# Dequantized FFN weights in a macaron block: gate and up weights by bytes, 1024 wide in PSUM, low halves on VectorE, gathers in sections of 1, 4 and 6 tiles

## The reference

```python
def _dequant(qw, qz, sc, g_idx):
    shifts = jnp.arange(8, dtype=jnp.uint32) * 4
    wq = qw[:, None, :] >> shifts[None, :, None] & NIB
    wq = wq.reshape(-1, qw.shape[1]).astype(jnp.float32)
    zq = qz[:, :, None] >> shifts[None, None, :] & NIB
    zq = zq.reshape(qz.shape[0], -1).astype(jnp.float32) + 1.0
    return sc[g_idx] * (wq - zq[g_idx])
w_gu = _dequant(qweight_gu, qzeros_gu, scales_gu, g_idx_gu)      # 512 x 2752
inter = jnp.einsum('bsh,hf->bsf', x, w_gu)
gate, up = (inter[..., :INTER], inter[..., INTER:])              # INTER = 1376
h = jax.nn.silu(gate) * up
w_d = _dequant(qweight_down, qzeros_down, scales_down, g_idx_down)
return jnp.einsum('bsf,fh->bsh', h, w_d)

x = x + 0.5 * ffn(layernorm(x))
x = x + attention(layernorm(x))
x = x + 0.5 * ffn(layernorm(x))
```

## Time and profile before

| what | value |
|---|---|
| median of 3 runs (lowest, highest) | 660.63 us (659.92, 666.45) |
| profiled execution, its own time | 665.29 us |
| its span, first to last instruction | 663.5 us |
| TensorE busy, share of the span | 583.2 us, 88% |
| VectorE, ScalarE, GpSimd busy | 384.8, 281.8, 86.1 us |
| mean granted TensorE clock | 0.969 |

### The profile page before, as it was taken

The page is one execution under the profiler, slowest core; times in us unless marked ns, Lnnn a source line. Parts: engine busy times, 40 slices in busy tenths (PEclk is TensorE's granted clock), DMA queues, the critical chain, the costliest instruction groups (busy, mean ns, idle before and its releaser), DMA issues.

```text
span 663.5 us, 8621 instructions
## 1 busy us (share of the span) xinstructions
PE 583.2 (88%) x3024; PEld 439.4 (66%) x3024; DVE 384.8 (58%) x886; ACT 281.8 (42%) x816; POOL 86.1 (13%) x87
## 2 busy tenths in 40 slices
PE   1087988889999997797898898888999999999998
PEld 1065866658888885574574575545588887888886
DVE  7377999982331138889879979999121133411113
ACT  2132223231112135888998999799211111211111
POOL 4777545430000000000000000000000000000000
PEclk9997999998999999696999998989999999999999
DMA  6967334229600001103002001100590000100001
GB/s 165 285 194 215 109 99 127 76 76 277 296 1 1 0 1 32 33 1 64 2 1 56 9 1 33 34 0 2 160 331 1 1 0 1 64 0 1 0 1 64
DMA packets 44627, 46.71 MB, mean 70 GB/s; under 512 B 12636, under 2 KB 37318, under 8 KB 43816
## 3 DMA queue, kind: packets, MB, share of 16 engines
q1 hardware_dynamic: 39888, 35.51, 18.3%
q0 software_dynamic: 2656, 10.57, 5.3%
q10 hardware_dynamic: 2040, 0.08, 0.2%
HBM read 31.72 MB, written 10.30 MB: 63 GB/s over the span
## 4 chain that ended last, share of the span: by engine, by line
PE 61%; DVE 20%; ACT 6%; issue 6%; POOL 5%; ACTq 1%; DMA 0%; DVEq 0%; POOLq 0%
PE bank L1023 29%; PE bank L1038 14%; PE bank L1139 4%; DVE sc L861 4%; PE bank L1105 3%; DVE wf L700 3%; PE bank L1069 3%; ACT sc L560 3%; POOL zs L397 2%; DVE raw L690 2%; DVE wf L704 2%; DVE qp L832 2%; DVE nmax L870 2%; PE bank L1123 1%; ACT pt L575 1%
## 5 line engine op out<-in xcount | busy, mean ns | idle before, releaser
L712 DVE TENSOR_TENSOR hf<-sil,bank 128x512 f32<-128x512 f32 (+1 forms) x44 | 30.1, 685 | 178.9 <-PE bank L1023 178.9
L1038 PE MATMUL bank<-w_d,hs 128*128 128x512 f32 (+1 forms) x528 | 130.1, 396 | 2.1 <-ACT hs L496 1.3
L560 ACT ACTIVATE sc<-sc,nmax 128x128 f32<-128x128 f32 (+1 forms) x256 | 114.1, 451 | 21.4 <-DVE nmax L870 21.3
L1038 PEld LDWEIGHTS bank<-w_d,hs 128*128 128x128 f32 (+1 forms) x528 | 100.3, 191 | 24.1 <-ACT hs L496 1.5
L1023 PE MATMUL bank<-xt,w_far 128*128 128x512 f32 (+1 forms) x384 | 92.3, 394 | 5.9 <-POOL w_far L429 5.9
L1023 PE MATMUL bank<-xt,w_mid 128*128 128x512 f32 x384 | 90.6, 390 | 2.5 <-POOL w_mid L429 2.5
L1023 PE MATMUL bank<-xt,w_near 128*128 128x512 f32 x288 | 72.2, 410 | 21.6 <-POOL w_near L429 21.6
L1023 PEld LDWEIGHTS bank<-xt,w_far 128*128 128x128 f32 (+1 forms) x384 | 69.1, 181 | 26.7 <-issue 8.7
L861 DVE SCALAR_TENSOR_TENSOR sc<-dist,bank 128x128 f32<-128x128 f32 (+1 forms) x256 | 75.7, 347 | 17.6 <-PE bank L1091 9.2
L1023 PEld LDWEIGHTS bank<-xt,w_mid 128*128 128x128 f32 x384 | 71.7, 188 | 18.6 <-issue 3.9
L488 ACT ACTIVATE sil<-bank 128x512 f32<-128x512 f32 (+1 forms) x44 | 26.3, 597 | 129.3 <-PE bank L1023 129.3
(11 more groups left out here) (89 smaller groups left out, 569.6 us busy)
## 6 DMA issues: line engine op xcount, KB each, us to landing
raw<-in_L_ffn_qweight_gu SPq DMA_DIRECT2D x80, 64.0 KB, 2.7
gate_up_part<-w_mid SPq DMA_DIRECT2D x1, 4096.0 KB, 15.2
qp<-qp SPq DMA_DIRECT2D x8, 512.0 KB, 4.1
w_mid<-gate_up_part SPq DMA_DIRECT2D x4, 1024.0 KB, 8.9
gate_up_part<-w_far SPq DMA_DIRECT2D x1, 3840.0 KB, 23.8
w_far<-gate_up_part SPq DMA_DIRECT2D x3, 1024.0 KB, 9.1
raw<-in_L_ffn_qweight_down SPq DMA_DIRECT2D x10, 256.0 KB, 3.2
x<-in_L_attn_hidden_states SPq DMA_DIRECT2D x8, 256.0 KB, 4.1
```

Source lines behind the costliest of these rows:

```text
L560: ins = nc.scalar.activation(r, r, ACT.Exp, bias=nmax[:, n % 4, h:h + 1], accum_out=sums[:, g % 2, first + h:first + h + 1])
L712: nc.vector.tensor_tensor(hf[0:jw(j), n % 2, :], sil[0:jw(j), n % 2, :], up_ps[0:jw(j), :], ALU.mult).then_inc(h_ok, 1)
L1038: ins = nc.tensor.matmul(acc[t][:, :], hs[0:jw(j), n % 2, a, t * P:(t + 1) * P], w_d[0:jw(j), j, b, :], start=(j == 0 and q == 0), stop=(j ...
```

## The change

It does five things.

1. The gate and up contraction is reordered: partition 64e+r holds contraction rows 8r+2k+e. A packed word row then goes to two partitions instead of eight, and one shift by 0 or 4 with the mask 0x0f0f0f0f leaves four 4-bit numbers as the four bytes of a word, one for each contraction tile k. `xn_tile` writes the normalised tokens in that order (a read with a stride of 8 elements).
2. Gate and up weights of a tile are one chunk of 128x1024, held in a PSUM tensor of two banks (`wide`), instead of two of 128x512 in SBUF. Down chunks keep their size and have their own buffers.
3. The low halves are subtracted by VectorE (`gu_low`, `d_low`), not by GpSimd.
4. The sections have 1, 4 and 6 tiles instead of 3, 4 and 4. GpSimd issues all gathers in one row, the scales of a section ahead of its zeros, and waits for nothing of the dequantization.
5. In stage 0 the transposes go to banks 0 to 3, since 6 and 7 hold the products.

```diff
-    SEC = (0, 3, 7, NJ)
+    SEC = (0, 1, 5, NJ)
+            def load_raw(j):
+                if j >= 3:
+                    sp.wait_ge(gu_w, j - 2)
+                for e in range(2):
+                    src = bass.AP(qw_gu.tensor, j * P, [[2 * F, D // 8], [F, 2], [1, jw(j)]])
+                    dst = raw[64 * e:64 * e + 64, j % 3, 0:2 * jw(j)].rearrange("p (g n) -> p g n", g=2)
+                    sp.dma_start(dst, src).then_inc(raw_in[j % 3], 16)
...
-            pool.wait_ge(gi_in, 48)
+            pool.wait_ge(gi_in, 32)
             groups(slice(0, KT), G_GU)
+            st.wait()
+            pool.wait_ge(s_ok[0], 16)
+            gather(0)
+            pool.wait_ge(gi_d_in, 32)
             groups(slice(KT, KT + NJ), G_D)
             st.wait()
-            pool.wait_ge(rows_ok[0], 32)
-            gather(0, 0)
-            gather(0, 1)
             pool.wait_ge(d_rows_ok, 32)
             gather_down(0)
...
+            for n in (1, 2):
+                gather_down(2 * n - 1)
+                pool.wait_ge(s_ok[n], 16)
+                gather(n)
+                gather_down(2 * n)
+            for j in range(5, NJ):
+                gather_down(j)
...
-            dq_high(0)
-            dq_high(1)
+            gu_high(0)
             for j in range(NJ):
                 if j + 1 < NJ:
-                    dq_high(3 * j + 2)
+                    gu_high(j + 1)
                 silu(0, j)
...
+                h_high(0, j)
+                if j + 1 < NJ:
+                    d_high(j)
...
+            def gu_weight(j):
+                n, cols = section(j)
+                dve.wait_ge(raw_in[j % 3], 32 * (j // 3 + 1))
+                words = raw[:, j % 3, 0:2 * jw(j)]
+                st.did(nc.vector.tensor_scalar(words, words, shifts[:, 0:1], low4[:, :].bitcast(I32),
                                                ALU.logical_shift_right, ALU.bitwise_and))
+                dve.wait_ge(gathered[n], 128)
+                if j >= 1:
+                    dve.wait_ge(gu_lo, j)
                 st.wait()
+                q = words.bitcast(U8).rearrange("p (g n k) -> p k g n", g=2, k=KT)
+                w = gu_product(j)
+                st.did(nc.vector.scalar_tensor_tensor(out=w, in0=q, scalar=1.0, in1=zs[n][:, :, :, cols],
+                                                      op0=ALU.subtract, op1=ALU.subtract))
                 st.wait()
+                nc.vector.tensor_tensor(w, w, gu_weights(0, j).bitcast(F32), ALU.mult).then_inc(gu_w, 1)
+            def gu_low(j):
+                dve.wait_ge(gu_hi, j + 1)
+                nc.vector.tensor_tensor(gu_weights(1, j), gu_product(j), gu_weights(0, j).bitcast(F32),
+                                        ALU.subtract).then_inc(gu_lo, 1)
...
             for j in range(NJ):
-                dequant(3 * j + 2)
                 if j + 1 < NJ:
-                    dequant(3 * j + 3)
+                    gu_weight(j + 1)
+                    h_mul(0, j)
+                    d_weight(j)
+                    gu_low(j + 1)
+                    h_low(0, j)
+                    d_low(j)
                 else:
+                    d_weight(j)
                     for t in range(2):
                         xt_low(1, t)
                         ffn_xn(1, t + 2)
-                h_mul(0, j)
-                if j + 1 < NJ:
-                    dequant(3 * j + 4)
-                h_low(0, j)
+                    h_mul(0, j)
+                    d_low(j)
+                    h_low(0, j)
...
-                    if s == 0 and gu == 0 and k % 2 == 0:
-                        pe.wait_ge(w_hi, chunk_no[j, k // 2] + 1)
-                        pe.wait_ge(w_lo, chunk_no[j, k // 2] + 1)
+                    if s == 0 and gu == 0 and k == 0:
+                        pe.wait_ge(gu_hi, j + 1)
+                        pe.wait_ge(gu_lo, j + 1)
```

More of the change, by code:

```diff
@@ L147, in macaron_block @@
     with ctx:
-        bank = [ctx.enter_context(nc.psum_tensor(f"bank{n}", [P, 512], F32)) for n in range(8)]
+        bank = [ctx.enter_context(nc.psum_tensor(f"bank{n}", [P, 512], F32)) for n in range(6)]
+        wide = ctx.enter_context(nc.psum_tensor("bank6_7", [P, 1024], F32))
+        bank += [wide[:, 0:512], wide[:, 512:1024]]
         acc = bank[0:4]
@@ L277, in chunk_of, with gu_product, d_weights, tr_bank @@
[L277 to L282 removed]
+            return w_sec[n][:, part, :, :, cols]
+        def gu_product(j):
+            return wide[:, 0:8 * jw(j)].rearrange("p (k g n) -> p k g n", k=KT, g=2)
+        def d_weights(part, j):
+            return w_d[0:jw(j), j, part, :]
+        def tr_bank(s, t):
+            return bank[t] if s == 0 else bank[6 + t % 2]
@@ L999, in ffn_transposes @@
             def ffn_transposes(s, t):
-                if t >= 2:
+                if s == 1 and t == 0:
+                    pe.wait_ge(gu_lo, NJ)
+                if s >= 1 and t >= 2:
                     pe.wait_ge(xt_lo, 4 * s + t - 1)
-                transposes(tile_no("ffn", s, t), bank[6 + t % 2])
+                transposes(tile_no("ffn", s, t), tr_bank(s, t))
             PARTS = ((0, 0), (1, 0), (0, 1))
```

233 lines of the change are left out of this document (104 added, 129 removed).

## The result

| | this kernel | before, measured beside it | ratio, 95% interval |
|---|---|---|---|
| first measurement | 676.37 us (674.35 to 677.67, 4 runs) | 663.06 us (659.92 to 666.45, 4 runs) | 1.0197 [1.0128, 1.0267] |

The forecast was 659.7 us with a range of 652 to 671: the change was forecast as no difference and measured 2% slower (1.3 to 2.7% by the interval). The profiled execution took 674.35 us, its span 671.8, at a mean granted clock of 0.966, against 665.29, 663.5 and 0.969 before.

What follows compares the result with a forecast made beforehand. Stage 0 was taken as bound by the wait for GpSimd's first low half, then by VectorE in the rounds. Its -1.4 us and +0.5 elsewhere made -0.9 on a median of 660.6: 659.7 us, range 652 to 671 (8 in 10).

Steps and rivals of the forecast that it cites:

- the start: Stage 0 up to `h_mul` of tile 1: tile 1's rows there at 34.0 us, its gate at 43.4, `h_mul` at 51.2.
- The -0.9: Whole kernel: -1.4 us in stage 0 and +0.5 elsewhere, laid on a median of 660.6 to give 659.7 us.
- First gather at 6.5: GpSimd at the start: index loads landed at 5.5 us, groups take 1.0, so the first gather starts at 6.5.
- My upper end of 7.7: GpSimd at the start: at worst its first group computation still waits for index loads until 7.7 us.
- Chain from the rows to the second gate: From tile 1's rows at 34.0 us through dequantization and tile 0's h to tile 1's gate at 43.4.
- Rounds: Stage 0, tile to tile: 9.55 us, 10.3 in the four with moments, 10.9 with the reciprocal root's seed.
- The rival of the falling clock: Stage 0 rounds: TensorE's idle gaps drop its clock in 8 to 9 rounds, about +15, 674 us; chance 14%.
- End of stage 0: From tile 10's gate and up to the last down product: 5.8 us against 7.4, beginning at 146.8, 1.4 earlier.
- Elsewhere +0.5: Between stages 2 and 3 and in the attention: `xn_tile`'s strided read takes 0.69 us instead of 0.54, +0.5 in all.
- The refill was hidden: Stage 2: tile 1's refill lands at 480.5 us, needed at 482.8, so hidden with 2 us to spare, cost 0.
- Stages 1 to 3: taken as equal: Later stages: TensorE runs almost without a gap from stage 1 on; no change summed beyond the +0.5 elsewhere.
- the largest part of my chance: Whole kernel: chance 0.48 of no difference within one per cent, 6.6 us; 0.24 below 654, 0.28 above 667.2.

Runs made afterwards that it cites:

- e10: Changed kernel with sections of 3, 4 and 4 tiles and 2 x 18 extra matmuls around tile 0 to keep TensorE busy: 676.56 us, 1.0164 of before.
- e2: Changed kernel with 30 extra matmuls on TensorE right behind gate and up of tile 0: 665.68 us, 1.0017 of before.
- e8: Changed kernel with the rows of down tile 4 gathered ahead of the far section instead of behind it: 669.11 us, 1.0035 of before.
- e9: Changed kernel with twelve unused DRAM to DRAM copies beside the far gathers: 676.33 us, 1.0171 of before.
- e12: Changed kernel, unedited, as the control of series 3: 674.90 us, 1.0153 of before.
- e14: Changed kernel with GpSimd's far-section gathers and down rows paced by waits: 668.06 us, 1.0066 of before.
- e15: Changed kernel with the down rows alone paced by waits: 668.18 us, 1.0061 of before.
- e17: Changed kernel with sections of 3, 4 and 4 tiles and all gathers behind the first section's paced: 665.90 us, 1.0019 of before.
- e18: e17 with down tile 3's rows asked for earlier and the 36 extra matmuls of e10 around tile 0: 660.08 us, 0.9936 of before.
- e5: Changed kernel, unedited, run again as the control of series 2: 668.76 us, 1.0043 of before.
- e13: Changed kernel, unedited, as a control in series 4 and 5: 668.02 us, 1.0060 of before.
- e19: Changed kernel, unedited, as a control in series 4 and 5: 668.05 us, 1.0049 of before.
- e3: Changed kernel with the old sections of 3, 4 and 4 tiles: 663.53 us, 0.9993 of before.
- e7: Changed kernel with one extra matmul behind gate and up of tile 0: 668.40 us, 1.0036 of before.
- e6: Kernel before with only the sections changed, to 1, 4 and 6 tiles: 666.16 us, 0.9986 of before.
- e4: Changed kernel with tile 0's h ahead of tile 1's weights in VectorE's and ScalarE's lists: 664.75 us, 0.9994 of before.

## Why the forecast was wrong

**The failed step is the start: "So `h_mul` of tile 1 starts at 43.4 + 5.64 + 2.2 = 51.2".** It came at 60.05. Of the 8.85 us, 1.35 are the gathers (below) and 6.4 the late answer to up of tile 0. The late answer to gate of tile 1 adds 0.9: the rest of its 3.04 us passes while TensorE is still at that tile's up, until 59.13. The last 0.2 are small terms. I had taken for granted, from a trace in which it always held, that a finished matmul is seen at once. In the first measurement it was not, for up to 11.6 us.

Shown about that stall: it is no property of the program alone. The same kernel took 676.4 and 674.9 us in two measurements and 668.8, 668.0 and 668.1 in three; with it `h_mul` of tile 1 stands at 58.5 to 60.5, without it at 52.6 to 53.2. It goes by series, and so far by chip: of the four chips one had it in all four kernels, the other three in none. Since the stalling chip had one series only, chip and occasion can't be told apart. The kernel before shows no sign of it in its times, 660 to 668 throughout; a trace of it was taken once, without the stall. It is not the idle TensorE (e10), not the exact program (e2 to e8 against e9 to e12), not the section sizes (e10 has the old ones), and it ends within about 1 us of the last gather's packets in four of five traces. Only argued: that the gathers without a pause are its cause, which e14, e15, e17 and e18 would have told on a chip that has it; that wasn't to be had. What is held back (the semaphore's write, the matmul's completion, TensorE's supply of instructions, or all of it by the recording, as every run here was recorded) is open too.

**The base of the forecast was low.** The -0.9 was laid on a median of three runs, 660.6; the 115 runs of the same kernel in the five series have a median of 665.8. From there the same forecast would have read 664.9.

**The rest of the forecast, by e5,** where the stall is absent:

- *First gather at 6.5: wrong by 2.2 to 2.5.* The later index load still landed at 7.2 to 7.5, and the two took a median of 4.6 to 4.9 us from their issue, not 3.4: the load's 2 KB are now two transfers in a new layout. GpSimd in the changed kernel (first measurement), its first group computation and its first gather:

```profile
7.58 0.25 POOL L383 TENSOR_SCALAR gneg<-gidx 128x4 int32<-128x4 int32 x1 [4.93 <-DMA gidx<-in_L_ffn_g_idx_gu]
...
9.00 1.21 POOL L397 DMA_INDIRECT w_near<-scale_rows,gidx  x1 [0.61 <-POOL gidx L387]
```

  My upper end of 7.7 was the right value. The last middle gather started at 31.95 (29.4), its rows landed 3.0 to 3.4 later (4.6): 35.4 for 34.0. That is +1.4 of `h_mul` tile 1's 52.8.
- *Chain from the rows to the second gate:* 9.45 for 9.4, cold products 7.85 for 7.84. Right.
- *Rounds:* 9.65 twice, then 10.36 three times for 9.55 and 10.3; 11.1 with the seed for 10.9. Right in kind, about 0.1 short each, 1 us over nine. One round took 11.3, because the clock fell there: gate and up in 7.38, in a window (83 to 90 us) at a granted clock of 0.79. The rival of the falling clock was real in one round of nine, not in all. Of the other traces of this kernel e13 and e19 had one such round too, the first measurement and e12 none; e3 and e8 had two, e7 none.

```profile
86.34 7.38 PE bank L1060 x24
```

- *End of stage 0:* last down product 5.8 behind gate and up of tile 10; 5.84 in the changed kernel (151.03 to 156.87). Right. Not in the sum: this product now runs warm, 2.97 us, where it took 5.46 before. I had read that it was slow before (among the rivals), and did not ask whether it still would be. It gives 2.5 us back by itself and 2.9 with what follows: between `h_mul` of tile 10 and the next stage's first, 13.57 us before, 10.66 now. The chain of the changed kernel:

```profile
151.03 0.45 PE bank L1030 x4
...
156.08 0.70 DVE hs L746
...
156.87 2.97 PE bank L1075 x12
```

- *Elsewhere +0.5:* from stage 1's last `h_mul` to stage 2's first, with the attention between, 243.15 us before, 243.9 to 244.8 after; between stages 2 and 3, 13.19 and 13.61. So +1.2 to 2.0. `xn_tile` takes 0.74 (median) where I took 0.69. The refill was hidden, as said: the first round of stage 2 takes 5.4 us in both kernels, and the stage from `h_mul` of tile 1 on 73.88 before and 74.11 now.
- *Stages 1 to 3: taken as equal, +0.6.* From first to last `h_mul` they take 0.17, 0.23 and 0.22 us more (e5). It goes with the sections: the kernel before has the same with sections of 1, 4 and 6 tiles (e6), the changed one with 3, 4 and 4 (e3) has not. Why is open.

In sum, without the stall: +3.8 up to the last down product against forecast (1.4 gathers, 1.0 clock, 1.0 rounds, the rest handovers), less 2.9 for the warm product, plus 0.7 to 1.5 more elsewhere than the 0.5, plus 0.6 in stages 1 to 3. From -0.9 that makes +1.3 to +2.1; the spans differ by 1.6, the medians of the three series without the stall by 2.1 to 2.7, 0.4 to 0.6%. That is within 1%, where the largest part of my chance lay, but on the other side of zero, and the closeness is in part luck: +3.8 and -2.9 cancel, and neither was in the sum. The first measurement's 676 is that and the stall.

**Where the change loses what it wins.** e3 takes the old sections and is even with before (0.9993); the change as it is loses 0.4 to 0.6%. The small first section brings tile 0 hardly sooner: the eight gathers cost their 1.25 us of issue whatever their rows' length, and tile 0's gate starts at 27.5 to 28.7 us in all but one of the traces with one tile in it (29.2 in e4), at 28.5 to 29.4 in the four with three. That 1 us buys nothing, since VectorE has tile 1's product ahead of `h_mul` of tile 0, and tile 1 now stands behind eight more gathers: its `h_mul` comes at 52.8 (e5) against 49.1 (e3). The sections are not the only way back: e4, with the small sections but tile 0's h first, is even with before as well (0.9994), and so is e2 with 30 matmuls more (1.0017). In the kernel before the sections don't matter (e6), since its first low half waited for GpSimd's queue anyway.

## What to carry to other kernels

An indirect gather here cost GpSimd its 1.25 us of issue whatever its bytes, so a first section smaller than what the second tile needs bought 1 us where it didn't count and lost 3.6 where it did. Ask of each matmul group near an edit what clock it will run at, in both directions: the two cold products at the start cost some 4 us, and 3.7 of these were to be had back with 36 matmuls that compute nothing (e18 against e17), and a warm one at the end gave 2.5 us that nobody had asked for. Before building on a single measurement's ratio of 2%, take the same kernel again on another chip: here that took away three quarters of the difference.
